# Closing the phases of a four-part transformer kernel without GpSimd's drain

## The reference

```python
x = x + attn_a(layernorm(x), Wq, Wk, Wv, Wo)          # 16 heads of 16, causal
x = x + ffn(layernorm(x), norm_scale, gate_w, ...)    # 8 experts, the best 2 of each row
x = x + attn_b(layernorm(x), w_qkv, w_fc, ...)        # one head of 256, then a layer norm
x = x + ffn(layernorm(x), norm_scale, gate_w, ...)

def ffn(x, ...):
    t = x * rsqrt(mean(x * x) + eps) * norm_scale
    logits = t @ gate_w + gate_b                      # top 2, softmax over these
    for each expert e:
        y += w[:, e] * (swiglu(t @ w1[e] + b1[e]) @ w2[e] + b2[e])
    return x + y
```

## Time and profile before

| | us |
|---|---|
| time, median of 3 runs | 1918.77 (1917.91 to 1919.66) |
| the profiled execution's own time | 1919.07 |
| its span, first to last instruction | 1917.3 |
| PE busy | 1725.4 (90%) |
| DVE, ACT, POOL busy | 1314.6, 842.5, 789.2 |

### The profile page before, as it was taken

One profiled execution on the slowest core, in us unless ns is written; L12 is line 12 of the kernel. 1 busy time (PEld: TensorE's weight loads), 2 busy tenths in 40 slices (PEclk: granted clock), 3 DMA queues, 4 the chain that ended last, 5 costly groups with the idle time before them and its releaser, 6 DMA issues. The chain is left out here.

```text
span 1917.3 us, 32412 instructions
## 1 busy us (share of the span) xinstructions
PE 1725.4 (90%) x8300; PEld 957.7 (50%) x8301; DVE 1314.6 (69%) x2668; ACT 842.5 (44%) x1706; POOL 789.2 (41%) x771
## 2 busy tenths in 40 slices
PE   6969999999999686799999999599974999999997
PEld 3533343434343275466666666344543566666664
DVE  4638887878787077676777777258876677777774
ACT  3423666756566453333333333347763333333332
POOL 4330111111111122366666665315442566666663
PEclk9977999999999897799999999799975999999998
DMA  4662544424251256222322223400114322222222
GB/s 132 161 143 69 123 102 104 114 85 116 83 123 57 69 178 230 70 44 44 47 47 44 44 45 43 108 1 23 52 58 144 59 46 44 44 47 46 44 44 30
DMA packets 104673, 148.96 MB, mean 78 GB/s; under 512 B 18128, under 2 KB 86736, under 8 KB 101520
## 3 DMA queue, kind: packets, MB, share of 16 engines
q1 hardware_dynamic: 68176, 102.35, 19.5%
q0 software_dynamic: 31808, 37.32, 12.4%
q10 hardware_dynamic: 4608, 8.39, 1.2%
HBM read 82.54 MB, written 56.69 MB: 73 GB/s over the span
## 5 line engine op out<-in xcount | busy, mean ns | idle before, releaser
L512 DVE TENSOR_REDUCE a_mx<-a_p_sn 128x1 f32<-128x512 f32 (+3 forms) x640 | 371.8, 632 | 92.4 <-PE a_p_sn L551 62.5
L485 ACT ACTIVATE a_Pt<-a_p_st 128x512 f32<-128x512 f32 (+2 forms) x624 | 307.1, 577 | 195.2 <-PE a_p_st L565 179.3
L1270 ACT ACTIVATE e_y<-e_yb,wt 128x256 f32<-128x256 f32 x142 | 72.2, 508 | 510.2 <-DVE e_yb L1297 510.2
L1230 PE MATMUL e_p_y<-w,e_hT 128*128 x1136 | 271.0, 382 | 2.0 <-ACT e_hT L1264 2.0
L1209 PE MATMUL e_p_g<-values_then_w,e_tT 128*128 x568 | 270.7, 600 | 0.0
L1209 PE MATMUL e_p_l<-values_then_w,e_tT 128*128 x568 | 268.3, 595 | 0.0
L1230 PEld LDWEIGHTS e_p_y<-w,e_hT 128*128 128x128 f32 x1136 | 216.9, 191 | 92.0 <-issue 65.1
L548 PE MATMUL a_p_sn<-Kst,Qst 96*128 96x512 bf16 (+3 forms) x768 | 249.2, 345 | 8.1 <-DMA Qst<-qk_parts 5.5
L461 POOL TENSOR_SCALAR_AFFINE_SELECT a_Pt<-a_Pt 128x512 f32<-128x512 f32 x128 | 81.5, 637 | 423.5 <-ACT a_Pt L485 423.5
L565 PE MATMUL a_p_st<-Qst,Kst 99*128 99x512 bf16 (+3 forms) x768 | 216.0, 334 | 16.8 <-ACT a_Pt L485 14.1
L1118 POOL DMA_INDIRECT xs<-t_rows,token x142 | 141.2, 994 | 100.1 <-DVE token L1056 48.2
(11 more groups left out here) (206 smaller groups left out, 2492.0 us busy)
## 6 DMA issues: line engine op xcount, KB each, us to landing
qk_parts<-a_part SPq DMA_DIRECT2D x64, 192.0 KB, 2.8
a_Vst<-values_then_w SPq DMA_DIRECT2D x16, 512.0 KB, 16.8
o_rows<-a_OT ACTq DMA_DIRECT2D x32, 256.0 KB, 2.1
values_then_w<-in_mlp SPq DMA_DIRECT2D x16, 512.0 KB, 3.5
t_rows<-R SPq DMA_DIRECT2D x16, 512.0 KB, 3.0
R<-in_mlp_b SPq DMA_DIRECT2D x16, 512.0 KB, 7.1
Kst<-qk_parts SPq DMA_DIRECT2D x16, 384.0 KB
Qst<-qk_parts SPq DMA_DIRECT2D x16, 384.0 KB
```

The costliest lines, as they stand in the source:

```text
L485: act.activation(weights(kb, slice(h, h + n), a, b), p_st[:, i % RING, 0:n * (b - a)].rearrange("p (n w) -> p n w", n=n), ACT.Exp, scale=D ...
L512: dve.tensor_reduce(mx[:, hs[0]:hs[-1] + 1, place], p_sn[:, (s + k) % RING, 0:w * len(hs)].rearrange("p (h w) -> p h w", w=w), AX.X, ALU.m ...
L1230: mm = pe.matmul(p_y[:, s, 0:D], hT[:, s, k * P:(k + 1) * P], g["w2"][:, bass.ds(e, 1), k, :].rearrange("p a n -> p (a n)"), start=(k == 0 ...
```

## The change

Six of the seven `nc.Block()` get an argument, that is all blocks that the program opens but the first: eight closings, since `rank` and `experts` are called twice.

```diff
@@ project_qkv
-    with nc.Block() as block:
+    with nc.Block(no_gpsimd_drain=True) as block:
```

## The result

Median 1909.38 us (1907.02 to 1911.18, 4 runs), against 1918.34 us (1916.56 to 1919.66, 4 runs) of the kernel before beside it: ratio 0.9963, interval [0.9948, 0.9978]. (The medians of these four runs alone stand at 0.9953.) Two later timings of the same kernel gave 0.9963 [0.9948, 0.9978] and 0.9971 [0.9959, 0.9983]. So the change makes the kernel faster by 0.3 to 0.4%, by the three pairs of medians 5 to 9 us. That is short of the 13.2 us of the sum; the median of 1909.38 lies inside the range (1902.8 to 1911.6). Over the 79 runs of the kernel before and the 28 of the changed kernel that have their clock on record (without one slow run of 7979.55 us) the means are 1916.7 and 1910.0 us, 6.7 us apart. The profiled execution took 1907.02 us.

A forecast was written before the change was run, and what follows sets the result against it. PE, busy for 90% of the span, was taken to bound the kernel, so only its idle stretches could give time back. Terms -5.7 - 5.7 - 1.0 - 1.0 + 0.2 = -13.2 us gave 1905.6 us, range 1902.8 to 1911.6.

The forecast's parts named there:

- The main case: Whole kernel: all terms together give -13.2 us, 1905.6 us, own range 1903.3 to 1909.3; chance 0.63.
- the paid end: Rival, behind the program's end: GpSimd's DMA queue must still come to rest, time 5.7 us longer, 1911.3 us; chance 0.09.
- the put-off work: Rival, second rank phase: the first gather after layer b pays the drain's 5.7 us, 1911.3 us; chance 0.06.
- Ends of the experts phases: Closings of both experts phases: GpSimd's bare DRAIN goes, everything behind moves up, -5.7 us each.
- Ends of the rank phases: Closings of both rank phases: barrier closes at DVE's arrival, tile 1 is turned earlier, -1.0 us each.
- at the head of the stream, so I take 3.0 us: Start of the experts phases: tile 1's weights, issued amid bias loads, land after 3.0 us; bounds 2.4 and 4.8.
- the rival of unharmed gathers: Start of the experts phases: tile 1's weights still land after 2.4 us, gains 1.7 and 1.6, 1904.3 us; chance 0.13.
- What is added: Four closings where GpSimd is early: one more event semaphore in the last arrival's path, +0.2 us, bounds 0.07 and 0.8.
- The clock: Whole kernel: counted as nothing, with 1 us put on each side of the range.
- No effect: Rival, at the closings: whatever instruction follows GpSimd's DMAs waits as long as the drain, 1918.8 us; chance 0.04.
- Slower by growing DMAs: Rival, second experts phase: without drains GpSimd's DMAs grow; 0.60 us more each gives 1926.9 us; chance 0.03.

The follow-up runs named there:

- bias_after_gathers: The changed kernel with SP holding the eight bias loads of an experts phase until tile 1's rows and weights have landed; 0.9927, 1902.21 us.
- ranks: The kernel before with only the two rank phases closing without GpSimd's drain; 1.0011.
- the fill: The changed kernel with some 2.2 us of needless GpSimd work before the first experts phase's closing, starting layer b later; 0.9952, 1908.72 us.
- last_experts: The kernel before with only the second experts phase closing without GpSimd's drain; 0.9971, 5.6 us faster.
- first_experts: The kernel before with only the first experts phase closing without GpSimd's drain; 0.9981, 3.6 us faster.
- experts_both: The kernel before with both experts phases, and no other blocks, closing without GpSimd's drain; 0.9945, 10.5 us faster.
- drain_probe: The changed kernel with drains put back behind tile 1's gathers in each rank phase and at layer b's closing; profiled once, drains 0.39 and 7.15 us.

## Why the prediction was right, and where its sizes were off

*The number.* It was met in part by luck. The main case's own range ends at 1909.3, and the 1909.38 lies just beyond; the room up to 1911.6 was made for two rivals, the paid end and the put-off work, and neither of them took its 5.7 us here. Set against the 1918.77 of the prediction, the later ratios would give 1911.7 and 1913.2 us, outside the range. (The lower end of the own range stands in the prediction once as 1903.3 and once as 1902.9; its terms give 1903.3.)

*Ends of the experts phases, -5.7 us each.* Right. r+e 1 is 6.0 us shorter with that edit alone, r+e 2 5.6 us with the other alone. The times follow with 5.6 us for the second and 3.6 us for the first, whose interval (1.1 to 6.1 us) holds 5.7.

*Ends of the rank phases, -1.0 us each.* Right in each step of the mechanism, mis-sized: the step "at the head of the stream, so I take 3.0 us" failed. Tile 1's weights took 3.9 us to land in both phases, inside the bounds of 2.4 and 4.8, and the terms were 0.2 and 0.0 us. With the bias loads held they landed in 2.3 us, and both r+e columns together fell by 3.5 to 3.7 us, where the rival of unharmed gathers had 1.7 + 1.6. The drain's own debt, which I didn't know of, takes 0.4 us back where the next drain is bare; in the changed kernel no drain follows. The barrier closed 0.2 to 0.3 us behind DVE, as forecast.

*What is added, +0.2 us.* Of that size. From the start of the last arrival's DRAIN to SP's release the closings of the projection, the attention, the output rows and layer b took 0.1, 0.1, 0.1 and 0.2 us before, and 0.2, 0.2, 0.3 and 0.2 us in the changed kernel, each rounded to 0.1 us. In the times it can't be told.

*The clock, nothing, with 1 us on each side.* The 1 us was an estimate that no run shows. What the traces show of the granted clock in its place are the levels 0.50 and 1.00, and 0.87 to 0.90 on the mean of layer b. The terms of the rank phases explain 1.8 us of the shortfall. The rest is larger, 2 to 6 us, and this is the one term of the sum left that could hold it. Layer b took 231.9 us before and 232.6 to 233.4 in three traces of the changed kernel. It differs by up to 6.5 us over the kernels, and all of that is in PE's speed. The whole of layer b in bias_after_gathers, in the kernel before and in the changed kernel, with the columns of the earlier trace rows:

```profile
1211.30:1438.50 227.20, 193.96 (x608) 105.04 (x608) 158.73 (x431) 135.50 (x255) 96.19 (x128) 0.90 0.18 59
```

```profile
1219.90:1451.80 231.90, 199.29 (x608) 107.56 (x608) 158.69 (x431) 135.52 (x255) 96.17 (x128) 0.88 0.18 58
```

```profile
1211.90:1445.30 233.40, 199.95 (x608) 107.56 (x608) 158.73 (x431) 135.56 (x255) 96.21 (x128) 0.87 0.18 57
```

PE runs the same 608 matmuls in 194.0, 199.3 and 200.0 us, at a mean granted clock of 0.90, 0.88 and 0.87, while DVE, ACT and POOL are busy for the same time within 0.1 us. The whole kernel does likewise: of the 79 runs of the kernel before, the 2 with a mean clock of 0.943 took 1910.6 us on the mean, the 18 with 0.939 1916.4, the 15 with 0.937 1919.6.

Rows of shorter stretches show where the clock falls. Stretches that begin 41 us and 78 us behind the release in front of layer b, in the changed kernel (233.4 us) and in ranks (229.5 us); the figure in the third column from the right is the granted clock:

```profile
1253.00:1260.00 7.00, 6.17 (x18) 3.13 (x19) 0.38 (x1) 2.92 (x8) 0.00 (x0) 0.76 0.00 0
...
1290.00:1304.00 14.00, 10.12 (x28) 4.88 (x26) 6.15 (x19) 11.26 (x23) 3.50 (x5) 0.76 0.00 0
```

```profile
1264.00:1271.00 7.00, 5.97 (x23) 3.42 (x24) 1.80 (x4) 3.73 (x9) 0.95 (x2) 1.00 0.00 0
...
1301.00:1315.00 14.00, 10.12 (x32) 4.94 (x31) 7.42 (x19) 11.50 (x26) 3.50 (x5) 0.88 0.00 0
```

In the changed kernel the clock falls to 0.50 for part of the 7 us (0.50 on the mean from 1256 to 1258), in ranks it stays at 1.00, and a second fall around 85 us is twice as deep in the first (0.76 against 0.88). In the first stretch PE, busy for 6.2 and 6.0 us, gets through 18 matmuls in the one and 23 in the other; 30 us later the two kernels stand at 175 and 176, so a lead in such a stretch says less than the sums above. So the traces show that layer b's length goes with PE's speed. That the change is what makes the clock fall more, they don't show. All six traces whose first experts phase closed without a drain, with neither the bias loads held nor the fill, lie at 232.6 to 233.7 us (three of them with 0.3 to 0.4 us of a drain's debt); the five with a drain there lie at 229.5 to 233.7.

*The rivals.* Gathers unharmed: out, by the 3.9 us. Paid at the end: out, by last_experts and by 1.7 us between time and span. Put off: nearly right as a mechanism, since the debt is real and survives; but only a drain collects it, no gather does, and the changed kernel has no drain left. No effect: out. Slower by growing DMAs: out, the page of the changed kernel has them as in the earlier trace rows:

```profile
L1118 POOL DMA_INDIRECT xs<-t_rows,token x142 | 141.1, 993 | 99.5 <-DVE token L1056 48.2
...
L1124 POOL DMA_INDIRECT wt<-pick_weights,pick x142 | 150.3, 1058 | 43.3 <-issue 43.3
L1181 POOL DMA_INDIRECT out<-e_y,result x71 | 115.3, 1623 | 123.6 <-ACT e_y L1270 123.6
```

*What stays open.* Terms as measured make -6.2 - 5.5 = -11.7 us, and layer b gives back 0.7 to 1.5 us, which leaves 10 to 11 us. The three timings say 5 to 9 us. One execution's trace can't tell whether the missing 1 to 6 us are more of layer b in the typical execution or lie in the attention, whose 518.6 to 524.7 us have no relation to any edit here that the traces show.

## What to carry to other kernels

A barrier that lets everybody go earlier also lets the next phase's loads go earlier (here SP's bias loads, 0.4 us behind DVE's arrival instead of 3.9): before taking a wait away, list what is queued right behind it and which small transfer on the critical path it will meet. Here one wait on SP that holds them back gave 3.5 to 3.7 us on top by the traces. GpSimd's drain at the end of a block had a price by its DMAs since the last drain (0.4 us for 4, 5.7 us for 209), and it showed only where GpSimd arrives last (5.7 us at the experts phases' closings, 0.3 us at layer b's). So look for it behind a long run of indirect DMAs that semaphores wait for anyway. Where a drain has to stay, it can be moved to a closing at which GpSimd is early: in first_experts all but 0.3 us of the 5.7 hid there. And look at the spread before trusting a gain of this size: the kernel before alone took 1910.1 to 1922.6 us.

## What the runs showed of the hardware that I had not expected

GpSimd's drain has a price by the DMAs since the last one: 0.04 us with none, 0.38 to 0.39 us with four, 5.72 us with 209, 6.10 us with 213. It is owed unchanged 230 us later (7.15 us less 1.5 us of arithmetic, in first_experts, experts_both and drain_probe). If no drain comes, nothing here collects it: the 426 DMAs of the changed program took 0.99, 1.06 and 1.62 us on the mean, before 0.99, 1.10 and 1.62, and the time behind the span didn't grow. The same instructions of layer b took 227.2 to 233.7 us, with PE busy for 194.0 to 200.8 us by its granted clock and the other engines for the same time.
